# One wide log and one wide root for two layer norms, and a loop that begins with the scores

## The reference

```python
# layer 0; windows of 4x4 pixels, 4 heads of 16
qkv = xw @ qkv_w.T + qkv_b
qn, kn = q / norm(q), k / norm(k)
attn = einsum('whnd,whmd->whnm', qn, kn) * scale + bias     # 16x16 for each window and head
attn = softmax(attn)
a = einsum('whnm,whmd->whnd', attn, v) @ proj_w.T + proj_b
x = x + layernorm(a, norm1_g, norm1_b)                       # (a - mean) / sqrt(var + 1e-5) * g + b
h = gelu(x @ fc1_w.T + fc1_b) @ fc2_w.T + fc2_b
x = x + layernorm(h, norm2_g, norm2_b)
# layer 1: trend = moving average over 25 rows; seasonal = x - trend;
#          128 Fourier modes of seasonal are mixed by a complex matrix for each channel
return trend + irfft(mixed modes)
```

## Time and profile before

| what | value |
|---|---|
| median of 3 runs | 8726.0 us (8725.6 to 8736.03) |
| the profiled execution's own time | 8730.04 us |
| its span, first to last instruction | 8728.2 us |
| mean granted TensorE clock | 0.971 of full speed |
| TensorE matmul busy | 8045.9 us, 92% |
| ScalarE, VectorE, GpSimd busy | 70%, 67%, 62% |
| layer 0's groups, about | from 0.27 to 7.47 ms |

### The profile page before, as it was taken

The page is one execution under the profiler, slowest core; times in us unless marked ns, Lnnn a source line. Parts: engine busy times, 40 slices in busy tenths (PEclk is TensorE's granted clock), DMA queues, the critical chain, the costliest instruction groups (busy, mean ns, idle before and its releaser), DMA issues.

```text
span 8728.2 us, 660309 instructions
## 1 busy us (share of the span) xinstructions
PE 8045.9 (92%) x293684; PEld 5316.4 (61%) x293684; DVE 5884.0 (67%) x8029; ACT 6123.9 (70%) x8530; POOL 5384.8 (62%) x5127
## 2 busy tenths in 40 slices
PE   8889999999999999999999999999999999778686
PEld 5556666666666666666666666666666665566565
DVE  1467777777777777777777777777777777222121
ACT  1468888888888888888888888888888888322121
POOL 0367777777777777777777777777777777000000
PEclk9889999999999999999999999999999999889888
DMA  3122222222222222222222222222222222799999
GB/s 99 51 48 58 57 57 57 58 57 57 56 58 58 57 57 57 57 55 55 57 58 58 57 57 57 58 57 57 56 58 58 57 56 55 239 316 323 331 316 334
DMA packets 1187112, 834.31 MB, mean 96 GB/s; under 512 B 633233, under 2 KB 1043217, under 8 KB 1182867
## 3 DMA queue, kind: packets, MB, share of 16 engines
q1 hardware_dynamic: 1182404, 698.61, 31.1%
q10 hardware_dynamic: 4608, 134.22, 3.6%
HBM read 412.97 MB, written 285.21 MB: 80 GB/s over the span
## 4 chain that ended last, share of the span: by engine, by line
PE 91%; issue 4%; DMA 4%; SPq 0%; ACT 0%; DVE 0%; ACTq 0%; POOL 0%; POOLq 0%; DVEq 0%
PE ps L501 15%; PE ps L479 14%; PE ps L542 12%; PE ps L554 11%; PE ps L462 10%; PE ps L581 10%; PE ps L526 6%; PE ps L513 6%; PE ps L450 3%; DMA out<-arena 3%; PE ps L424 1%; PE ps L415 1%; PE ps L416 1%; SPq L278 0%; ACTq L733 0%
## 5 line engine op out<-in xcount | busy, mean ns | idle before, releaser
L953 POOL TENSOR_TENSOR arena<-arena 128x512 f32<-128x512 f32 x1024 | 1044.9, 1042 | 896.8 <-PE ps L501 896.8
L479 PEld LDWEIGHTS ps<-arena 32*32 32x32 f32 x131072 | 1226.2, 106 | 509.9 <-issue 505.4
L501 PEld LDWEIGHTS ps<-arena 32*32 32x32 f32 x131072 | 1296.7, 103 | 287.5 <-issue 260.4
L501 PE MATMUL ps<-arena 32*32 32x16 f32 x131072 | 1426.2, 186 | 21.9 <-issue 20.5
L479 PE MATMUL ps<-arena 32*32 32x16 f32 x131072 | 1332.1, 180 | 25.4 <-issue 16.6
L985 POOL TENSOR_TENSOR arena<-arena 128x512 f32<-128x512 f32 x512 | 714.4, 1395 | 871.6 <-DVE arena L844 871.6
L805 DVE TENSOR_TENSOR arena<-ps,arena 128x768 f32<-128x768 f32 x1024 | 980.7, 958 | 365.6 <-PE ps L462 365.3
L542 PE MATMUL ps<-arena 64*128 64x512 f32 x4096 | 1033.2, 621 | 209.2 <-issue 206.7
L581 PE MATMUL ps<-xch,amat 128*128 128x256 f32 x4096 | 924.9, 389 | 287.2 <-ACT arena L718 196.2
L462 PEld LDWEIGHTS ps<-arena 64*128 64x128 f32 x8192 | 648.9, 188 | 837.0 <-issue 829.9
L694 ACT ACTIVATE arena<-ps,arena 128x1024 f32<-128x1024 f32 x1024 | 1131.9, 1106 | 6.7 <-PE ps L542 6.7
(11 more groups left out here) (89 smaller groups left out, 14246.7 us busy)
## 6 DMA issues: line engine op xcount, KB each, us to landing
arena<-in_x SPq DMA_DIRECT2D x4096, 32.0 KB
arena<-arena SPq DMA_DIRECT2D x1024, 128.0 KB
y<-ystripe SPq DMA_DIRECT2D x256, 512.0 KB
amat<-mix SPq DMA_DIRECT2D x512, 256.0 KB, 3.3
xch<-y SPq DMA_DIRECT2D x512, 256.0 KB, 4.0
out<-arena ACTq DMA_DIRECT2D x32, 4096.0 KB, 27.1
mix<-amat SPq DMA_DIRECT2D x64, 256.0 KB, 2.0
wri<-in_w_real SPq DMA_DIRECT2D x64, 64.0 KB, 1.8
```

Of the source, the lines that this page charges most:

```text
L479: ins = mm(S(sl)[r, c0 + e:c0 + 32:2], qT[r, sl, q, e:64:2], kT[r, sl, q, e:32:2], start=True, stop=True, tile_position=(32 * cg, 32 * cg))
L501: ins = mm(PV[32 * h:32 * h + 32, b, c0:c0 + N], vexp[r, sl, h, :, :], pT[r, sl, h // 2, h % 2, :], start=True, stop=True, tile_position=( ...
L953: tt(vexp.rearrange("p s h e d -> p (s h) e d")[:, :, e, :], qkv[ring(g, 4)][:, 2].rearrange("p s (h d) -> p (s h) d", h=HEADS), par[:, e: ...
```

## The change

Five things are changed.

1. TensorE's loop begins with the scores' first half. The two `first_layer` steps, which stood at the head of the body for group `i6`, stand at its end for `i5`. The cyclic order of TensorE's steps is the same; the loop's branch lies behind `first_layer` and no longer behind `weighted`.
2. `MA` and `MB` change places for all users.
3. `log1` and `log2` become one `logs` over the two variances at once (1024 columns), `root1` and `root2` one `roots`. The results lie side by side (`ls`, `rts`).
4. ScalarE: `root_norm` directly behind `log_norm`; `square1` behind the second gelu.
5. VectorE and GpSimd take other orders. On VectorE `invert` comes before `normed1`, `gain2` of an older group between `normed1` and `add1`, `normed2` behind `add1`, `turn_prob` and `clamp` ahead of `bias`. On GpSimd `add_o2` comes at the body's head, `divide` ahead of `add2`, `norm_k` ahead of `scale_norm`. `LAG` is 8 instead of 7, one more drain step.

```diff
-LAG = 7
+LAG = 8
-        VV = MB
+        VV = MA
-        XT = MB[:, 0, :]
+        XT = MA[:, 0, :]
...
-                first_layer(i6, 0, MB, fc1a_ps)
-                first_layer(i6, 1, MA, fc1b_ps)
                 scores(i2, 0)
                 project(i4)
                 turn_x(i0)
                 scores(i2, 1)
                 second_layer(i6, 0, fc2a_ps)
                 second_layer(i6, 1, fc2b_ps)
-                project_qkv(i0, 0, MA, qkvA_ps)
+                project_qkv(i0, 0, MB, qkvA_ps)
                 weighted(i3, 0, pvA_ps)
                 variances(i4, i6)
-                project_qkv(i0, 1, MA, qkvB_ps)
+                project_qkv(i0, 1, MB, qkvB_ps)
                 weighted(i3, 1, pvB_ps)
+                first_layer(i5, 0, MA, fc1a_ps)
+                first_layer(i5, 1, MB, fc1b_ps)
...
+                def logs(g, h):
+                    if there(g) or there(h):
+                        event(act, var_ps, g)
+                        lo, hi = 0 if there(g) else 512, 1024 if there(h) else 512
+                        f(ls[:, lo:hi], VV.rearrange("p a n -> p (a n)")[:, lo:hi], ACT.Ln, bias=eps).then_inc(logs_sb, 1)
+
+                def roots(g, h):
+                    if there(g) or there(h):
+                        event(act, logs_sb, g)
                         need(act, dn1_sb, before(g))
+                        need(act, dn2_sb, before(h))
+                        lo, hi = 0 if there(g) else 512, 1024 if there(h) else 512
+                        f(rts[:, lo:hi], ls[:, lo:hi], ACT.Exp, scale=-0.5).then_inc(roots_sb, 1)
...
-                sum_prob(i3)
-                turn_k(i2)
-                qkv_out(i1, 1, MA, qkvB_ps, qkvB_sb)
-                turn_q(i2)
                 normed1(i5)
+                gain2(i8)
+                add1(i5)
                 normed2(i7)
-                invert(i3)
-                add1(i5)
+                turn_prob(i3)
                 sum_squares(i1)
+                clamp(i1)
                 bias(i2)
-                turn_prob(i3)
-                clamp(i1)
                 maximum(i2)
-                gain2(i7)
-                qkv_out(i0, 0, MA, qkvA_ps, qkvA_sb)
+                qkv_out(i0, 0, MB, qkvA_ps, qkvA_sb)
+                sum_prob(i2)
+                turn_k(i1)
+                qkv_out(i0, 1, MB, qkvB_ps, qkvB_sb)
+                turn_q(i1)
+                invert(i2)
```

## The result

The changed kernel takes 8745.5 us (12 runs, 8732.3 to 8757.8), beside 8727.0 us for the kernel before on the same chip (12 runs, 8721.8 to 8738.7). The ratio is 1.002, 95% interval 1.0012 to 1.0028: slower, by about 0.2%. Forecast were 8704 us and a gain. The profiled execution took 8753.2 us at the same granted clock, 0.971.

A forecast was written before the change was run, and what follows sets the result against it. ScalarE's chain to `keep_o` was taken to bound TensorE, with x's load binding store groups. Gains of 46 us in ordinary groups, less 22 in store groups and 2 for the drain, gave 22 net: 8704 us, range 8640 to 8755.

The forecast's parts named there:

- The scores' slack behind `keep_o`: Before the change, ScalarE's `keep_o` ended so near the scores' start that only 0.05 us was spare, from 0 to 0.1.
- the other orders: Reordered steps on VectorE, GpSimd and ScalarE (`root_norm`): costed at nothing, covered by idle stretches.
- a free x: Rival: x's load ends with room to spare in store groups, all 495 groups gain 0.125 us, 8666 us; chance 0.15.
- TensorE setting the pace: Rival: ordinary groups win the whole 0.41 us hole ahead of `first_layer`, 8576 us; chance 0.06.
- a long wait for the log: Rival: root starts 0.10 us after the log, 8726 us (chance 0.14); at 0.20, 8763 us (slower: chance 0.15).
- The store group: Every fourth group, storing a stripe of y: late x makes `turn_x` to `turn_x` 14.08 us against 13.89, losing 0.19.
- 0.08 to notice it: Store group: time between x's arrival and `turn_x`, added to 14.00 us to make 14.08.
- the ordinary group: Group without a store: gains 0.05 + 0.095 - 0.02 = 0.125 us, 46 us over 371 groups.
- The scores now start with an empty queue: TensorE's scores after waiting for `keep_o`: slower by 0 to 0.29 us, taken as 0.02.
- `square1` behind the second gelu: ScalarE: `square1` done 1.15 us after `turn_x`'s start, before 0.89; harmless in ordinary groups, 0.19 us lost in store groups.
- The rest of the loop: TensorE from scores to next `variances`: keeps its order, with only the 0.02 us for the empty queue charged.
- the held chain: `variances` through ScalarE's `keep_o` to the scores: forecast to shorten from 5.57 to 5.43 us.

## Why the forecast was wrong

**What held by its own steps.** `keep_o` holds the scores in every group: the distance between its end and them is 0.144 us throughout, forecast 0.15. From the first log to the table load it is 2.241 us on the mean (before 2.321): the wide pair gained 0.080 us, forecast 0.095; the root waits 0.05 us for the log, forecast 0.04. The scores' slack behind `keep_o` was 0.09 us before on the mean, forecast 0.05. The estimate from the Trainium skill, "ScalarE: Activation LUTs", section "What ACT_TABLE_LOAD costs", was 2.19 for the pair; it held no wait between log and root, and with the 0.05 it is the measured 2.24. (The "0.02 us more gained" behind it doesn't follow from its own numbers.) The Trainium skill's rule in "Perfetto Trace Analysis", section "Optimizing Scalar/DVE Operations", that breaking instructions up may help, found no support: two versions without and with the merging, 8454.8 and 8458.8 us, are alike. `variances` to scores: 5.61 to 5.44 us, forecast 5.57 to 5.43. TensorE is held 0.32 us on the mean, forecast 0.2. The steps behind the other orders, costed at nothing, hold as well. The rivals of a free x, of TensorE setting the pace, and of a long wait for the log did not come about.

**The store group** came out at 13.98, forecast 14.08, but the kernel before stood at 13.93 on the mean and not at the 13.89 of the one group I read. `square1` was done 1.058 us after `turn_x` (forecast 1.15, before 0.887), and x landed 12.78 us after the swap (forecast 12.83). Its "0.08 to notice it" stood in no row; it is 0.12 from the landing to `turn_x`. `turn_x` waits 0.22 us in the mean of these groups. Up to the scores the store group gained 0.305 us, since there its second `weighted` and the hole had been 0.12 longer than in the others; it lost 0.137 in the scores and 0.219 in the wait. That makes +0.051, where +0.19 was forecast (and 0.18 stands in the sum, 1 us in all).

**The step that failed** is the ordinary group, forecast to gain 0.125 us and found to lose 0.036. Three terms:

1. "The scores now start with an empty queue ... I take 0.02, near the low end, because one such row proves little." It measures 0.077 in the ordinary groups, 0.092 over all. Outside the group behind the store, the half takes 1.23 to 1.31 us, by version and place, where TensorE waited for `keep_o`, and 1.195 where nothing held it. The single row with 1.56 was a poor guide: it stands right behind a store (the store's x is issued from 4422.88 to 4430.96), beside loads at 45 GB/s, and in that place this half took 1.35 us on the mean even before. In the other groups of the kernel before, none but one was held by over 0.05 us, so they could not price it. That it is the queue, that is, the weight loads that can't run ahead during the wait, is argued. Shown is that it doesn't come without the wait: the branch alone is not it (1.195 with the branch in the same place and no wait), nor are x's loads (1.28 with the small ones). But every version with waits over 0.1 us also has the branch ahead of the scores, so whether a wait alone would do is open. With the loop turned back, 29 ordinary groups held by 0.01 to 0.1 us took 1.29 and the others 1.21; in the kernel before, 14 groups held by as little took 1.21, like the rest. In the trace it is one pause behind the eighth of the half's 128 records, in some groups and not in others.
2. "`square1` behind the second gelu ... In an ordinary group nothing minds." Not so: `square1` ends 0.2 us later in two of the three (1.08 us after `turn_x`, not 0.88; behind a late `turn_x` it ends at 0.70), and 0.7 us later where TensorE is not held (1.58), and the loads of x behind it lie otherwise beside the small products. Undoing this one order gives some 35 us here and some 80 us where TensorE is not held. This was the costliest blind spot: I followed who waits for a transfer and never who works beside it.
3. "The rest of the loop ... keeps its order", so it was priced at nothing. The scores behind the late `turn_x` of a store group take 0.105 us more; counted from `turn_x` to `turn_x` they belong to the ordinary group behind it, 0.035 us for the mean of the three. The first `weighted`, which stands on the held chain, takes 0.054 more in ordinary groups, 0.040 over all. Why it goes from 1.49 to 1.55, when it lies wholly beside the loads in both kernels, is not settled. It falls to 1.50 with `square1` first and to 1.33 without the full loads, so it belongs to them.

For the ordinary group that makes -0.127 for the held chain (forecast -0.145), +0.077, +0.035 and +0.054, together +0.039 where +0.036 was measured; over all groups -0.172 + 0.092 + 0.055 + 0.027 + 0.040 = 0.042 us, 21 us slower. The sign hung on terms of some 0.05 us that I had priced from single rows or left out.

## What to carry to other kernels

A hole on the busiest engine is worth nothing while a second chain ends just behind it; take that chain away first (here by moving a copy ahead of a table load that it did not need, and a store behind the load that is wanted sooner), and the same edit that was worth nothing brings 2.8%. When an edit moves the start of a transfer, ask what computes beside it, not only who waits for it: here runs of small products took longer beside the issuing of loads, and the profile counts that as busy time. The amount of traffic did not tell which ones. And read a duration in both cases, held and not held, as a mean over many groups that are alike in the rest: the single row here mixed a wait with a transfer and was off by more than the whole effect.

## What the runs showed of the hardware

- 64 small products (32x32 by 32x16) took 1.19 us in the second `weighted` without the full x loads, and on the mean 1.20 to 1.47 with them (256 KB in 8 DMAs, issued over some 6 us), longer the more of the issuing lay beside them, at the same rate of x, 44 to 54 GB/s. In the first `weighted`, measured to `variances`, it was 1.33 against 1.48 to 1.60; beside the store's 205 GB/s it was 1.34. The extra time is one or two pauses of 0.05 to 0.2 us. Products with results of 64x512 and 64x192 were not slower.
- The same products take 0.07 to 0.10 us more on the mean when TensorE had passed its loop's branch and then waited for another engine by 0.1 us or more just before.
- Waits of about 1.1 us for x in one group of four brought the granted clock from 1.00 to 0.50 behind 24 of 90 of them, 137 us together. Between 1.5 and 6.5 ms of the kernel before it fell once, for 3.4 us, and in the changed kernel not at all.
- A copy on ScalarE ran as fast ahead of the gelu table load as behind it: 0.61 us.
